# One adaLN block on one core: the prologue computes modulation by columns, spreads the first rows with TensorE and starts group 0 on several engines; the leads of the stages are shorter

## The reference, cut to what matters

```python
mod = (_silu(L0_c) @ L0_wmod).reshape(8, 6, 1, 512)
sa, ca, ga, sb, cb, gb = (mod[:, i] for i in range(6))
ga = (2 * (ga >= 0) - 1) * jnp.maximum(jnp.abs(ga), 0.25)   # gb alike
h = _layernorm(x) * (1 + ca) + sa
x = x + ga * attention(h)
h = _layernorm(x) * (1 + cb) + sb
x = x + gb * (dequant(quant(h)) @ dequant(quant(W)).T + bias)
```

## Time and profile before

| What | us |
|---|---|
| median of 3 runs (lowest, highest) | 393.85 (393.21, 394.97) |
| profiled execution, its own time | 395.14 |
| span of the profiled execution | 393.3 |
| first product of tile 0 starts | 77.04 |
| last addition starts | 388.46 |
| busy: PE, DVE, ACT, POOL | 323.8, 305.9, 219.8, 251.2 |

### The profile page before, as it was taken

One profiled execution on the slowest core, in us unless ns is written; L12 is line 12 of the kernel. 1 busy time (PEld: TensorE's weight loads), 2 busy tenths in 40 slices (PEclk: granted clock), 3 DMA queues, 4 the chain that ended last, 5 costly groups with the idle time before them and its releaser, 6 DMA issues.

```text
span 393.3 us, 6263 instructions
## 1 busy us (share of the span) xinstructions
PE 323.8 (82%) x2302; PEld 245.9 (63%) x2302; DVE 305.9 (78%) x500; ACT 219.8 (56%) x498; POOL 251.2 (64%) x137
## 2 busy tenths in 40 slices
PE   3940065458999999999899998979999989985995
PEld 0200012446899888688787776868887777764883
DVE  2892396589973699698979787999886899799733
ACT  2000954783743769587685969676874776211310
POOL 2005589994937959994998798698977782700000
PEclk9995559697999999999999999999998999999899
DMA  7996204159332505262442515232711961102032
GB/s 268 389 411 270 95 3 160 56 111 352 129 112 101 170 1 209 89 214 82 160 164 106 171 72 183 87 135 107 265 57 59 224 149 39 70 0 107 12 149 80
DMA packets 16772, 55.25 MB, mean 140 GB/s; under 512 B 2451, under 2 KB 2580, under 8 KB 12638
## 3 DMA queue, kind: packets, MB, share of 16 engines
q1 hardware_dynamic: 15846, 53.24, 39.5%
q10 hardware_dynamic: 896, 1.62, 1.2%
HBM read 37.65 MB, written 17.20 MB: 139 GB/s over the span
## 4 chain that ended last, share of the span: by engine, by line
PE 44%; DVE 31%; ACT 10%; issue 6%; DMA 5%; POOL 2%; ACTq 1%; SPq 1%; DVEq 0%; POOLq 0%
PE ps L571 8%; PE ps L572 8%; PE ps L576 8%; PE ps L554 4%; DVE DD L999 4%; DMA mod_scratch<-early 4%; DVE XL L962 3%; DVE amax L981 3%; PE ps L528 3%; PE ps L652 3%; DVE WL L969 3%; ACT unused L398 3%; PE ps L567 2%; DVE Q L992 2%; ACT U L390 2%
## 5 line engine op out<-in xcount | busy, mean ns | idle before, releaser
L571 PE MATMUL ps<-WH,XH 128*128 128x512 f32 x256 | 103.5, 404 | 1.1 <-ACT XH L374 1.1
L572 PE MATMUL ps<-WL,XH 128*128 128x512 f32 x256 | 103.0, 402 | 0.0
L326 POOL TENSOR_TENSOR U<-U,c_bc 128x1024 f32<-128x1024 f32 x32 | 76.5, 2390 | 39.3 <-ACT U L390 39.3
L317 POOL TENSOR_TENSOR X<-X,v_bc 128x1024 f32<-128x1024 f32 x32 | 75.5, 2383 | 36.8 <-DMA v_bc<-mod_scratch 36.8
L374 ACT ACTIVATE XH<-ps 128x512 fp32r<-128x512 f32 x64 | 37.9, 591 | 81.9 <-PE ps L554 81.7
L328 POOL TENSOR_TENSOR U<-U,sb_bc 128x1024 f32<-128x1024 f32 x32 | 76.7, 2397 | 2.5
L962 DVE TENSOR_TENSOR XL<-ps,XH 128x512 fp32r<-128x512 f32 x64 | 44.0, 688 | 41.8 <-ACT XH L374 41.7
L576 PE MATMUL ps<-WH,XL 128*128 128x512 f32 x256 | 69.0, 391 | 1.0 <-DVE XL L962 1.0
L390 ACT ACTIVATE U<-X,nmr,rstd 128x512 f32<-128x512 f32 x64 | 48.6, 808 | 25.4 <-DVE nmr L977 25.3
L398 ACT ACTIVATE unused<-X 128x512 bf16<-128x512 f32 x64 | 39.4, 619 | 36.8 <-POOL X L317 36.8
L572 PEld LDWEIGHTS ps<-WL,XH 128*128 128x128 f32 x256 | 49.8, 195 | 11.4
(11 more groups left out here) (208 smaller groups left out, 394.9 us busy)
## 6 DMA issues: line engine op xcount, KB each, us to landing
X<-in_x SPq DMA_DIRECT2D x16, 1024.0 KB, 5.4
out<-X SPq DMA_DIRECT2D x15, 1024.0 KB, 4.7
X<-in_wmod SPq DMA_DIRECT2D x4, 1024.0 KB, 9.5
v_bc<-mod_scratch SPq DMA_DIRECT2D x6, 256.0 KB, 5.0
c_bc<-mod_scratch SPq DMA_DIRECT2D x6, 256.0 KB, 5.1
sb_bc<-mod_scratch SPq DMA_DIRECT2D x6, 256.0 KB, 5.8
Wd<-in_w SPq DMA_DIRECT2D x1, 1024.0 KB, 12.7
U<-in_wmod SPq DMA_DIRECT2D x1, 1024.0 KB, 14.9
```

The source lines that it names most:

```text
L317: nc.gpsimd.tensor_tensor(a, a, spread(v_bc[:, b % 2, :]), ALU.add).then_inc(x1_done, 1)
L326: nc.gpsimd.tensor_tensor(a, a, spread(c_bc[:, b % 2, :]), ALU.mult).then_inc(u_done, 1)
L571: M(bank, XH[:, n % 2, r], WH[:, b % 2, k, :], start=False, stop=False)
L572: M(bank, XH[:, n % 2, r], WL[:, b % 2, k, :], start=False, stop=False)
```

## The change

- **Columns.** `modulation(i)` now has the wmod block as weights (16 loads of 128x128) and streams the 8 silu columns, so results stand as columns: 128 partitions by 4x8. `gate` works on 128x32. The table TA holds v, c, s, gb, gb*bias and ga as columns; `scale_weights` reads its factor there. The GB turn is gone.
- **Spread by TensorE.** `spread` multiplies a column, broadcast as weights, with the identity: the row on all partitions in PSUM. ScalarE copies it to v_bc, c_bc, sb_bc. DRAM serves only batches 2 and later for v, 1 and later for c and s. The order of DMAs is new: x 0 ahead of the weight, then the blocks. SyncE no longer loads G2 nor the eight msp pieces; G holds all batches' bias rows, high and low, and `pick` selects one.
- **Group 0 is split.** VectorE does the first half of group 0 itself, from PSUM (`x1_first`, `first_modulate`), GpSimd the second half. The weight's quantisation is split around the row scales.
- **Order by need.** The prologue is written out by hand on ScalarE and VectorE, with no loop from q=-17. Blocks 4 and 5 (ca, sa) are multiplied in `head_rows` at q=0 and q=1 of TensorE, on the head rows only. The bias rows move from the prologue to q=1 of VectorE, the centred diagonals to q=4. Head work is one tile later (BEGIN=9, AFTER=51), its last step not.
- **Shorter leads.** sums 9/8, deviations 8/7, normalise 6/5, scales 6, maxima 3 and 2 with the block scales by half, to_grid 3 and 1, from_grid 2 and 1. GpSimd: modulate(g), weights, add(g+2). The folds are four tiles in a row.

```diff
-BEGIN, PERIOD = 8, 15
-AFTER = 36 + 14
+BEGIN, PERIOD = 9, 15
+AFTER = BEGIN + 2 * PERIOD + 12
-    return k if b == 1 else 56 + k if b == B else 8 * b - 8 + (0, 1, 4, 5)[k]
+    return 56 + k if b == B else 8 * b - 5 + k
...
@@ sync @@
+            sp.dma_start(idf[:], ident).then_inc(small_in, 16)
             load_mod(0)
             load_x(0)
+            sp.dma_start(Wd[:], w.rearrange("(c p) k -> p c k", p=P)).then_inc(w_in, 16)
             load_mod(1)
+            load_x(1)
             load_mod(2)
             load_mod(3)
+            load_x(2)
+            load_mod(4)
             load_mod(5)
...
+            sp.wait_ge(mod_mm, 1)
+            load_x(3)
+            sp.wait_ge(rows_cp, 1)
+            sp.dma_start(mod_dram.rearrange("w b d -> (w b) d"), mod_rows).then_inc(scratch_out, 16)
+            sp.wait_ge(scratch_out, 16)
+            mod_row(c_bc[:, 1, :], 1, C, c_in[1])
+            mod_row(sb_bc[:, 1, :], 1, SB, sb_in[1])
+            sp.wait_ge(wt_mm, NC)
+            sp.dma_start(Wb[:], chunked(WqT)).then_inc(wq_in, 16)
+            sp.wait_ge(mod_mm, 5)
+            sp.dma_start(Wv[:], chunked(WvT)).then_inc(wv_in, 16)
+            sp.wait_ge(mod_mm, 6)
+            sp.dma_start(Wk[:], chunked(WkT)).then_inc(wk_in, 16)
+            load_x(4)
             load_x(5)
@@ gpsimd @@
+            add_attn_bias(0)
+            add_attn_bias(1)
+            scale_weights(0, Wfirst, 0, HALF)
+            scale_weights(0, Wfirst, HALF, NC)
+            modulate(0)
+            add_attn_bias(2)
+            scale_weights(1, Wsecond)
+            for g in range(1, GROUPS):
                 modulate(g)
                 if g % 2 == 1 and 3 <= g < GROUPS - 1:
                     scale_weights((g + 1) // 2, Wscaled)
+                if g + 2 < GROUPS:
+                    add_attn_bias(g + 2)
@@ scalar @@
+            spread_row(v_bc[:, 0, :], V0_BANK, v_mm, v_rows, 2)
+            sums(0, 0)
+            spread_row(v_bc[:, 1, :], V1_BANK, v_mm, v_rows, 3)
+            sums(0, 1)
+            for h in range(2):
+                deviations(0, h)
+            normalise(0, 0)
+            spread_row(c_bc[:, 0, :], C_BANK, c_mm, c_rows, 1)
+            normalise(0, 1)
+            spread_row(sb_bc[:, 0, :], S_BANK, s_mm, s_rows, 1)
+            sums(1, 0)
+            for k in range(NC):
+                weight_high(0, k, W_FIRST_BANKS[k])
+            act.wait_ge(rows_mm, 1)
+            A.copy(mod_rows, ps[0:ROWS * B, S_BANK, :]).then_inc(rows_cp, 1)
+            sums(1, 1)
+            high_part(0)
+            deviations(1, 0)
@@ tensor @@
+                for n in range(NC):
+                    for k in range(NC):
+                        m = M(mods(i)[:, n, :], mod_w[i][:, k, n * P:(n + 1) * P], cE[:, k, :],
+                              start=k == 0, stop=k == NC - 1)
+                m.then_inc(mod_mm, 1)
+            def spread(bank, which, b, signal):
+                for n in range(NC):
+                    m = M(ps[:, bank, n * P:(n + 1) * P], TA[:, n, which, b:b + 1].to_broadcast([P, P]), idf[:],
+                          start=True, stop=True)
+                m.then_inc(signal, 1)
...
+            modulation(1)
+            pe.wait_ge(gb_col, 1)
+            pe.wait_ge(v_rows, 1)
+            rows_of(GBIAS_BANK, GBIAS, GBIAS + 1, gbias_mm)
+            modulation(2)
+            pe.wait_ge(c_col, 1)
+            spread(C_BANK, C, 0, c_mm)
+            modulation(3)
+            pe.wait_ge(s_col, 1)
+            spread(S_BANK, SB, 0, s_mm)
@@ vector @@
+                link(TS(sign, mods(i), 0.0, 0.5, ALU.is_ge, ALU.subtract))
+                link(STT(size, sign, 2.0, mods(i), ALU.mult, ALU.mult))
+                link(TS(size, size, 0.25, 2.0, ALU.max, ALU.mult))
+                link(TT(size, size, sign, ALU.mult))
+                W_.tensor_copy(TA[:, :, dst, :], size).then_inc(dve_step, 1)
...
+            def centre_diagonals():
+                dve.wait_ge(bd_in, 16)
+                for n, i in enumerate((0, 2)):
+                    link(RED(bdm[:, n:n + 1], BD[:, i, :], AX, ALU.add))
+                    link(TS(bdm[:, n:n + 1], bdm[:, n:n + 1], 1.0 / HD, None, ALU.mult))
+                    for q in range(4):
+                        r = slice(32 * q, 32 * q + 32)
+                        link(TS(BD[r, i, r], BD[r, i, r], bdm[r, n:n + 1], None, ALU.subtract))
...
+            early_constants()
+            gate(0, GA, BO, V, v_col)
+            dve.wait_ge(v_mm, 1)
+            dve.wait_ge(x_in[0], 16)
+            TT(X1[:, 0, 0:HALF, :], X1[:, 0, 0:HALF, :], spread(V_BANK), ALU.add).then_inc(x1_first, 1)
+            dve.wait_ge(w_in, 16)
+            quantise(Wd[:, 0:HALF, :], Q8[:, 0], HALF * NB).then_inc(wd_done, 1)
+            gate(1, GB, BIAS, GBIAS, gb_col)
+            quantise_scales(Wd[:, HALF:NC, :], HALF * NB)
+            scales(0)
+            quantise_values(Wd[:, HALF:NC, :], Q8[:, 1], HALF * NB).then_inc(wd_done, 1)
+            dve.wait_ge(mod_mm, 3)
+            TS(TA[:, :, C, :], mods(2), 1.0, None, ALU.add).then_inc(c_col, 1)
+            gate_bias_rows()
+            dve.wait_ge(mod_mm, 4)
+            W_.tensor_copy(TA[:, :, SB, :], mods(3)).then_inc(s_col, 1)
+            first_modulate()
+            maxima(0, 0)
+            dve.wait_ge(wd_done, 2)
+            to_grid(0, 0)
+            from_grid(0, 0)
+            for k in range(NC):
+                weight_low(0, k, W_FIRST_BANKS[k])
+            low_part(0)
+            maxima(0, 1)
+            to_grid(0, 1)
+            from_grid(0, 1)
```

More of the change, by code:

```diff
@@ L356, in _ @@
             A = nc.scalar
+            act.dma_start(col[:], columns).then_inc(vec_in, 16)
+            act.dma_start(lrow[:], rows).then_inc(vec_in, 16)
+            act.dma_start(mk[:], masks).then_inc(mk_in, 16)
             act.wait_ge(c_loaded, 16)
@@ L491, in _ @@
                     weight_high(*FOLDS[q - 1], W_BANK)
+                if q == 0:
+                    deviations(1, 1)
+                    for h in range(2):
+                        normalise(1, h)
                 head_work(q)
                 for h in range(2):
-                    if (g := due(q, 9 - h)) is not None:
+                    if (g := due(q, 6 - h)) is not None and g > 2 or q == 3 and (g := 2):
                         normalise(g, h)
-                    if (g := due(q, 11 - h)) is not None:
+                for h in range(2):
+                    if (g := due(q, 9 - h)) is not None and g > 2 or q == 1 and (g := 2):
+                        sums(g, h)
+                for h in range(2):
+                    if (g := due(q, 8 - h)) is not None and g > 2 or q == 2 and (g := 2):
                         deviations(g, h)
-                    if (g := due(q, 13 - h)) is not None:
-                        sums(g, h)
         @block.tensor
@@ L532, in _ @@
             modulation(0)
[L533 to L546 removed]
+            pe.wait_ge(small_in, 16)
+            pe.wait_ge(v_col, 1)
+            spread(V_BANK, V, 0, v_mm)
+            spread(V0_BANK, V, 0, v_mm)
+            spread(V1_BANK, V, 1, v_mm)
+            pe.wait_ge(cleared, 2)
+            pe.wait_ge(rows_ok, 2)
+            M(blq_out, lrow[0:1, 0, :], ones[0:1, 0:1], start=True, stop=True).then_inc(blq_mm, 1)
+            modulation(1)
[8 more added lines that the diff above has]
+            spread(S_BANK, SB, 0, s_mm)
             def transposes(n):
@@ new lines, in first_modulate, with spread, gate_bias_rows @@
+            def first_modulate():
+                a = U[:, 0, 0:HALF, :]
+                dve.wait_ge(z_done, HALF)
+                dve.wait_ge(c_rows, 1)
+                TT(a, a, spread(C_BANK), ALU.mult).then_inc(u_first, 1)
+                dve.wait_ge(u_first, 1)
+                dve.wait_ge(s_rows, 1)
+                TT(a, a, spread(S_BANK), ALU.add).then_inc(h_first, 1)
+            def spread(bank):
+                return ps[:, bank, :].unsqueeze(1).to_broadcast([P, HALF, D])
+            def gate_bias_rows():
+                dve.wait_ge(cleared, 1)
+                dve.wait_ge(gbias_mm, 1)
+                row = ps[0:B, GBIAS_BANK, :]
+                W_.tensor_copy(G[0:B, :], row).then_inc(g_rows, 1)
+                dve.wait_ge(g_rows, 1)
+                TT(G[32:32 + B, :], row, G[0:B, :].bitcast(F32), ALU.subtract).then_inc(g_rows, 1)
```

431 lines of the change are left out of this document (190 added, 241 removed).

## The result

The changed kernel takes 409.12 us (median of 3 runs beside the kernel before, 407.03 to 411.47) against 393.79 us: a ratio of 1.039, 95% interval 1.0328 to 1.0452. The forecast was 377.5 us. Four executions that ran clearly slower than the others of their kernel, for reasons that stay open, are left out of every number here: 823.34 us of the changed kernel (with it the median is 410.30), 397.47 and 404.29 of the versions with the constants early and with streams, and 489.63 of the one with late constants and longer leads.

The account below looks back on a forecast made before the run. Bounds: a prologue, then VectorE to tile 6, then TensorE. Tile 0 earlier (-35.9), second stretch longer (+15.1), TensorE work owed (+4.5), rest zero: -16.3, so 377.5 us by the median; own range 370 to 383, whole range 362 to 386.

Parts of the forecast that it names:

- c column (0.2), G (1.4): 28.4: Prologue, VectorE taken as the chain: after the c column and G it would stand at 28.4 us.
- TensorE's order does: block 3 stands behind the spread of c (27.9), 3.3 us: 31.2: Prologue: TensorE's order, not block loads, binds; modulation block 3 follows the spread of c, takes 3.3 us, ends at 31.2.
- The second stretch: First product of tile 0 to that of tile 6, paced by VectorE: 51.7 us after the change, 36.6 before, +15.1.
- The hold-up: VectorE's bias rows (q=1) and centred diagonals (q=4) wait for GpSimd instructions at the shared SBUF ports: +6.0 and +9.0 us.
- so the rest is unchanged: zero, hidden behind its 261.5 of 275.1 us: From tile 6 on TensorE has the same work and is the bound, so the change there costs zero.
- the owed 4.5: At tile 6 TensorE still owes the v projection (3.6) and two weight turns (0.44 each), formerly done by then: +4.5 us.
- (b): Rival: short leads make ScalarE's sums wait for GpSimd's addition; 2 us more per group, 13 groups cost 26: 404 us; chance 0.04.
- (c): Rival: a smaller short-lead loss, one us per group, or TensorE at 1.2 GHz for longer: 383 to 391 us; chance 0.10.
- (a): Rival: little port hold-up of VectorE by GpSimd, tile 6 at 78 to 84 us: 362 to 369 us; chance 0.24.
- (d): Rival: the prologue does not shorten because another chain (landing of blocks, GpSimd's weights) was the real one: about 394; chance 0.02.
- If tile 0 starts past 48: Sign that the forecast is wrong: tile 0 starting past 48 us, where its first product was expected at 39 to 44.
- the hold-up rows: Sign: LR subtractions and casts and BD TENSOR_SCALARs on VectorE take 1 to 2.5 us, each ending just behind a GpSimd instruction.

Follow-up runs that it names:

- the last experiment: Version with early constants and VectorE's grid stages one tile earlier, its modulation blocks 2 and 3 replaced by 512-column products giving batch 0's rows already spread: 372.61 us, ratio 0.9458.
- the streams run: Version with early constants, plus 512-column products into an unused bank: ten before block 0, two behind each of a block's first three column groups: 399.83 us, ratio 1.012.

## Why the prediction was wrong

**The first stretch: the price of the blocks and spreads.** The step that failed is the sum behind "c column (0.2), G (1.4): 28.4" and "TensorE's order does: block 3 stands behind the spread of c (27.9), 3.3 us: 31.2". Block 3 ended at 43.8 us, 12.6 of the 14.9 us late. The bounds for a block were right, 3.6 and 7.2, but I took 5.0 for the first and 3.3, under my own lower bound, for block 3, and let blocks 1 and 2 lie behind VectorE's work at no price; they took 7.0, 4.1, 6.8 and 6.8. The spreads, priced at 0.9 each, took 5.5 for three and 2.1 for the others. By these the chain goes over from VectorE to TensorE, as VectorE's waits of 3.10 and 7.50 us show. (VectorE's own terms to "28.4" add up to 27.7; that slip is small beside these.) The old projection of 32 records ran in a stretch at the high clock and I carried its 0.11 us a record into a prologue whose mean clock was 0.75. The run with half blocks shows blocks 1 to 3 on the path for most of their length (7.6 of 9.2 us), and the run with batch 0 streamed, which replaces blocks 2 and 3 and their spreads, brings tile 0 forward by 8.5; block 0 is on it too in the changed kernel, where the gate follows it at once (7.59 + 6.97 = 14.56, gate at 14.68), but was not tested by itself.

**The second stretch: right.** 52.3 us against 51.7. The hold-up was 5.8 and 7.5 us for a forecast of 6.0 and 9.0, at the named instructions. Moving them away gave 15.7 us at tile 6 and 18.3 in all, for 18.6 of hold-up and own work; as a part of the gain comes from the clock behind tile 6, the near agreement of the last two is partly luck.

**The third stretch: "so the rest is unchanged: zero, hidden behind its 261.5 of 275.1 us".** This was the dearest step, and it had put the last stages' shorter leads at nothing: 16.8 us beyond the owed 4.5. From the windows: TensorE is busy 274.2 us instead of 261.5, 12.6 more, of which 4.5 are owed and the other 8.1 can only be slower steps, as the work is the same; and idle 22.0 instead of 13.5, 8.5 more. The average hid what happens at the start of a group, seven times here: the stages that stand last before TensorE come late, as they moved from leads of 3 and 2 tiles to 2 and 1. With DD one tile ahead, any addition or head row that VectorE takes first is paid by TensorE, and the clock behind it is paid again. Two runs show it from both sides: the kernel before with the short leads loses 15.3 us, the changed kernel with early constants gains 13.8 when nothing but these stages moves back by one tile.

**The rivals.** (b) had the cause, the leads, and nearly the time (404), with a chance of 0.04; but it priced the wrong link. It followed the longest chain, GpSimd's addition to ScalarE's sums, found 6 us to spare and stopped; the shortened link nearest to TensorE was not walked at all. That its 404 lies near the 409 measured is luck. By (c), "a smaller loss of that kind, or TensorE at 1.2 GHz for longer", one us per group would have been 13; measured 16.8. (a) and (d) were wrong: the hold-up was there, and the prologue did shorten by 21 us. The range ended at 386 because it took half of (c) beside a prologue taken as certain; by my estimate, with the upper price of the blocks (7.2 us each, block 3 some 12 us later) and one us for each of 13 groups, it would have passed 400.

**The signs named in advance.** "If tile 0 starts past 48" came true (56.05), "tile 6 at 90 to 95" did not (108.4), "TensorE busy for 95% from there" neither (274.2 of 296.2, 93%), and the hold-up rows looked as described.

## What to carry to other kernels

Where a schedule gives each stage a lead, walk every shortened link, the last one before the busy engine first: one tile of slack there was worth 13.8 us, and one more tile upstream nothing. An operation that was free because its engine waited is worth leaving in that wait: the constants cost nothing ahead of the first gate, and 18.3 us in the tiles beside GpSimd. Price short matmuls in a prologue at the pace that the prologue's own rows show, and prefer a few products of 512 columns that give the result in its final layout to many of 8 and a second pass to spread it.

## What the runs showed of the hardware that was not expected

The windows of the changed kernel's blocks 0 and 3:
```profile
7.60:14.60 7.00, 6.96 (x32) 6.86 (x32) 1.26 (x8) 0.00 (x0) 0.00 (x0) 1.00 1.00 368
...
37.00:43.80 6.80, 6.80 (x33) 6.73 (x32) 0.00 (x0) 2.00 (x3) 2.35 (x1) 0.50 0.00 0
```
The first block, behind 7.6 us of idleness, has a granted clock of 1.00 in the record and yet the pace of the block at 0.50, 0.21 us a record; block 1 took 4.07 us, 0.13 a record, at 0.90. So in the first microseconds the granted clock did not tell the pace. In the last experiment eight steps of 512 columns took 3.60 us at a granted clock of 1.00 with 8 output rows as with 128: there the number of rows that come out cost nothing.

The clock fell while TensorE was busy without a gap. In the changed kernel it fell at 25.1 us, within block 1, with TensorE busy since 16.04; in the streams run at 9.6 us, with TensorE busy since 7.23, and from 28.2 to 37.6 us it was busy all 9.4 us at 0.50. In the last experiment the clock rose from 0.50 to 1.00 at 31.4 us, within the first eight steps of 512 columns, which is why they took 5.25 us and the next eight 3.60. Why it falls where it does stays open.
